# Cross-attention on one core: x exchanged a group earlier, first loads split, GpSimd's cutting of the weights put behind its norms

## The chip, the core and the metric

The kernel runs on one core of a Trainium2 chip, as one launch. The metric is device time in microseconds (us). The engines are TensorE (PE in the profile, its weight loads PEld), VectorE (DVE), ScalarE (ACT), GpSimd (POOL) and SyncE (SP, which here only issues DMAs). They run side by side and wait for one another on semaphores.

## What is computed

Two decoder layers with the norm behind each residual. The change touches the second stage alone:

```python
x = layernorm(x + self_attn(x))          # stage A
# cross-attention, 32 query heads on 8 key heads of width 16, keys = values = ctx_512
qh = x.reshape(4, 512, 8, 4, 16);  kh = vh = ctx_512.reshape(4, 512, 8, 16)
w  = softmax(einsum('bkgsd,bktd->bkgst', qh, kh) / 4)
x  = layernorm(x + einsum('bkgst,bktd->bkgsd', w, vh))   # stage B, this change
x  = layernorm(x + ffn(x))               # stage F: weights cut to -1, 0, 1 by their mean size
```

Stage B has 4 batches of 512 tokens. Beside its own work it prepares the weights of stage F: their mean absolute size is summed, and each weight is compared with half of it.

## The kernel before

`stage_cross_attention` works in 32 groups: 4 batches (b) of 8 key heads (j), a group being the 4 query heads of one key head. `plan` is one list, written out by loops, that PE, ACT and DVE all follow.

- Start of a batch's queries: PE turns x (units `xt`, two halves), ACT rounds the turned half to `XTH`, DVE takes the rest to `XTL`. SP writes both to DRAM (`XP`, `unload_x`) and reads them back stacked into 48 rows of `QS` (`stack_queries`, six DMAs a group). This is the exchange of x. Keys go the same way, once per half batch: `CH`, `CL` to `CP`, then into `KS` (`stack_keys`, six DMAs).
- A group g has 8 `max` units of group g+1 or g+2 (PE product, DVE reduce L921), one `mt` unit (PE turns the maxima, DVE copies them to `mT` at L930, SP puts them as a row into `QS` by `shift_row`), 16 score products `S` (L1001), each followed by an exp on ACT (L870), four products with the values `P`, and a `turn` unit by which DVE divides and writes the output `Z`. The first `S` of a group waits for the row of its `mt` (`shifted`).
- `M` has two buffers and `T` three, so that PE, DVE and ACT hold one another in step.
- The norm of a batch: GpSimd adds x to `Z` (L830), DVE makes the moments (four `bn_stats` and 25 small steps, two taken behind each `max` unit by `next(pending)`), then GpSimd applies them (L833). The last batch is done by DVE alone at the end (L949 to L953).
- GpSimd also cuts the weights in 12 chunks (`cut_weights`: L817, L818, L822, then a DMA to `ffn_w`). The order on GpSimd is that of its program: chunks 0 and 1, sum and norm of batch 0, chunks 2 to 6, sum and norm of batch 1, chunks 7 to 11, sum and norm of batch 2. The stage ends when every engine has ended, and stage F begins behind a barrier.
- At the start SP loads the context in two DMAs, waits for ACT and DVE, writes `CP` and `XP`, waits for both, and then stacks keys and queries. PE waits at its top for four memsets of GpSimd (`ones_set`).

Of the kernel before, what the change touches and what calls it, by code (L numbers as in the profile page):

```python
# [4 lines left out]
F32 = mybir.dt.float32  # L5
# [4 lines left out]
ALU = mybir.AluOpType  # L10
ACT = mybir.ActivationFunctionType
# [584 lines left out]
def stage_cross_attention(nc, X, C, A, FW):  # L596
# [21 lines left out]
    with ctx:  # L618
# [78 lines left out]
        drained = lambda kind, arg: at[kind, arg] + 3  # L697

        block = ctx.enter_context(nc.Block())

        @block.sync
        def _(sp):
            sp.dma_start(CT[:], A["ctxT"].rearrange("b e s -> e b s")).then_inc(ctx_in, 16)
            sp.dma_start(CTOK[:].rearrange("p (b i) e -> p b i e", b=NB),
                         A["ctx_512"].rearrange("b (i p) e -> p b i e", p=P)).then_inc(tok_in, 16)

            def unload_x(b):
                sp.wait_ge(hi_done, 2 * b + 2)
                sp.dma_start(XP[b % 2][0], XTH[:].bitcast(F32)).then_inc(x_out, 16)
                sp.wait_ge(m_free, drained("xt", (b, 1)))  # L710
                sp.dma_start(XP[b % 2][1], XTL[:].bitcast(F32)).then_inc(x_out, 16)
                sp.wait_ge(x_out, 32 * (b + 1))

# [8 lines left out]

            def stack_keys(b, lo, hi):
                for r in range(2):
                    for n, part in enumerate((0, 1, 0)):
                        rows = slice(LOW * r + HD * n, LOW * r + HD * (n + 1))
                        src = CP[part][HD * lo:HD * hi, b, :].rearrange("(j d) s -> d j s", d=HD)
                        sp.dma_start(KS[rows, lo:hi].bitcast(F32), src).then_inc(keys[lo], 16)

            def shift_row(g):  # L730
# [5 lines left out]

            sp.wait_ge(ctx_hi, 1)
            sp.dma_start(CP[0], CH[:].bitcast(F32)).then_inc(ctx_out, 16)
            sp.wait_ge(ctx_lo, 1)
            sp.dma_start(CP[1], CL[:].bitcast(F32)).then_inc(ctx_out, 16)  # L740
            unload_x(0)
            sp.wait_ge(ctx_out, 32)
            sp.wait_ge(ones_set, 4)
            stack_keys(0, 0, 4)
            stack_queries(0)
            stack_queries(1)
            stack_keys(0, 4, 8)
            stack_queries(2)
            shift_row(0)
            for g in range(GROUPS):  # L750
                b, j = g // KV, g % KV
                if g >= 1:
                    sp.wait_ge(t_full, STEPS_S * g)
                if j == 5 and b + 1 < NB:
                    unload_x(b + 1)
                    stack_keys(b + 1, 0, 4)
                if g + 3 < GROUPS:
                    stack_queries(g + 3)
                if j == 0 and b >= 1:
                    stack_keys(b, 4, 8)  # L760
                if g + 1 < GROUPS:
                    shift_row(g + 1)

        @block.gpsimd
        def _(pool):
# [25 lines left out]

            def sum_weights():
                fetch(0)
                fetch(1)
# [43 lines left out]
        @block.scalar  # L838
        def _(act):
            act.wait_ge(ctx_in, 16)  # L840
            ac.activation(CH[:], CT[:], ACT.Copy).then_inc(ctx_hi, 1)
            act.sem_inc(t_free, 3)
            act.sem_inc(o_free, 1)
            act.wait_ge(tok_in, 16)
            act.wait_ge(ones_set, 4)

            def make_values(b):
                if b >= 2:
# [5 lines left out]
            make_values(0)  # L854
            for x in plan:
                if x[0] == "M" and x[1] == "xt":
                    b, half = x[2]
                    act.wait_ge(m_full, at["xt", x[2]] + 1)
                    if b >= 1:
                        act.wait_ge(x_out, 32 * b)  # L860
                    ac.activation(XTH[:, 2 * half:2 * half + 2, :].rearrange("p k s -> p (k s)"),
                                  M[at["xt", x[2]] % 2][:], ACT.Identity).then_inc(hi_done, 1)
                elif x[0] == "S":
                    g, s = x[1:]
                    if g % KV == 6 and s == 0 and g // KV + 1 < NB:
                        make_values(g // KV + 1)
# [3 lines left out]
                    ac.activation(PT[:, s // 4, head(s), :], T[(STEPS_S * g + s) % 3][:], ACT.Exp, scale=SCALE).then_inc(t_free, 1)  # L870
                    if g < 6 and s % 4 == 2:
                        piece = 4 * g + s // 4
                        c, half = piece // 2, piece % 2
# [11 lines left out]
        @block.vector  # L885
        def _(dve):
            dve.wait_ge(ctx_hi, 1)
            ve.tensor_tensor(CL[:].rearrange("p b s -> p (b s)"), CT[:].rearrange("p b s -> p (b s)"),
                             CH[:].bitcast(F32).rearrange("p b s -> p (b s)"), ALU.subtract).then_inc(ctx_lo, 1)
            dve.sem_inc(m_free, 2)  # L890
            step = Steps(dve, norm, 0, GROUPS + 1 + NT)
# [14 lines left out]
            for n, x in enumerate(m_units):  # L906
# [3 lines left out]
                if kind == "xt":  # L910
                    b, half = arg
                    dve.wait_ge(hi_done, 2 * b + half + 1)
                    if b >= 1:
                        dve.wait_ge(x_out, 32 * b)
                    ks = slice(2 * half, 2 * half + 2)
# [3 lines left out]
                elif kind == "max":  # L919
# [4 lines left out]
                    if delay < 0:  # L924
                        next(pending, None)
                        next(pending, None)
                elif kind == "mt":
                    if arg >= 1:
                        dve.wait_ge(shifted, 32 * arg)
                    ve.tensor_copy(mT[:, :], m[0:4 * NT, 0:P]).then_inc(m_free, 1)  # L930
                elif kind == "turn":
                    o = m[:, 0:S].rearrange("p (i h d) -> p i h d", i=NT, h=4)
# [11 lines left out]
                    if j == KV - 1:  # L944
                        delay, pending = 5, layernorm_moments(b)

# [11 lines left out]
        def _(t):  # L958
            t.wait_ge(ones_set, 4)
            for x in plan:  # L960
                if x[0] == "M":
# [1513 lines left out]
```

## Time and profile before

| | |
|---|---|
| median of 3 runs | 2573.51 us (2572.28 to 2574.54) |
| the profiled execution | 2594.45 us |
| its span | 2592.7 us |
| PE, DVE, ACT, POOL busy | 2025.5, 1739.4, 1247.0, 771.5 us |

The busy times are over the whole kernel; stage B is the stretch from 486.96 us (its first instructions) to 1049.66 us (DVE's last norm). A row of the timeline gives the start, the duration of the merged instructions, the engine, the line, what it writes and reads, how many there are, and in brackets how long the engine was idle before and what ended that. The names of stage B's tiles begin with `x_`. Times between two rows of the same kind show the pace of the groups.

### The profile page before, as it was taken

The numbers are of one execution on the slowest core, as the hardware profiler recorded it, in microseconds if no ns is written. First come the engines' busy times: TensorE is split into PE (matmuls) and PEld (weight loads), VectorE is DVE, ScalarE is ACT, GpSimd is POOL, SyncE is SP. The second block draws the span as 40 slices with busy tenths as digits, with TensorE's granted clock in tenths as the row PEclk, the third lists the DMA queues.
The fourth block names the chain that finished last, engine by engine and source line by source line (L and its number), as shares of the span: only waits on it lengthen the run. The fifth ranks groups of instructions, "written<-read, shape, count | busy, mean of one in ns | idle before, by whom it ended". The sixth has DMA issues, their size and how long they took to land. (4 is left out here: it accounts for less than half of the span.)

```text
span 2592.7 us, 33108 instructions
## 1 busy us (share of the span) xinstructions
PE 2025.5 (78%) x12220; PEld 1362.0 (53%) x12252; DVE 1739.4 (67%) x2695; ACT 1247.0 (48%) x2228; POOL 771.5 (30%) x872
## 2 busy tenths in 40 slices
PE   5999999377778787688887499999940479889990
PEld 4777787222222222355554378787830357667760
DVE  3546565376767675789997445556659855379986
ACT  2233232167555556367777423223229541178971
POOL 1111213201594950121110121122315204055525
PEclk8899999678888989899997689999975789889995
DMA  5332322456343420400000332223210030099966
GB/s 154 82 74 50 74 50 50 142 143 175 86 142 88 143 59 7 185 1 1 1 1 1 98 73 65 56 53 74 50 65 1 0 117 1 4 408 423 414 276 194
DMA packets 84591, 264.62 MB, mean 102 GB/s; under 512 B 17504, under 2 KB 19040, under 8 KB 73424
## 3 DMA queue, kind: packets, MB, share of 16 engines
q0 software_dynamic: 29632, 151.50, 17.5%
q1 hardware_dynamic: 53776, 110.75, 15.1%
q8 instruction: 99, 1.62, 0.3%
q14 instruction: 60, 0.49, 0.1%
q10 hardware_dynamic: 1024, 0.26, 0.0%
HBM read 169.87 MB, written 41.72 MB: 82 GB/s over the span
## 5 line engine op out<-in xcount | busy, mean ns | idle before, releaser
L921 DVE TENSOR_REDUCE x_negm<-x_M 128x2 f32<-128x1024 f32 x256 | 309.4, 1224 | 112.8 <-PE x_M L981 112.2
L870 ACT ACTIVATE x_PT<-x_T 128x512 f32<-128x512 f32 x512 | 279.9, 598 | 201.5 <-PE x_T L1001 196.3
L327 ACT ACTIVATE L_attn_PT<-L_attn_T 128x512 f32<-128x512 f32 x320 | 175.5, 595 | 359.0 <-PE L_attn_T L559 359.0
L409 DVE TENSOR_REDUCE L_attn_negm<-L_attn_M 128x2 f32<-128x1024 f32 (+1 forms) x192 | 192.1, 1041 | 57.2 <-PE L_attn_M L540 57.1
L234 POOL DMA_DIRECT2D L_attn_QKS<-L_attn_HL x64 | 34.8, 544 | 599.0 <-ACT L_attn_HL L312 565.1
L1001 PE MATMUL x_T<-x_QS,x_KS 49*128 49x512 f32 x512 | 141.1, 548 | 64.5 <-ACT x_PT L870 44.9
L557 PE MATMUL L_attn_T<-L_attn_QKS 97*128 97x256 f32 (+3 forms) x512 | 166.2, 386 | 8.4 <-DMA L_attn_QKS<-L_attn_mT 6.1
L1001 PEld LDWEIGHTS x_T<-x_QS,x_KS 49*128 49x128 f32 x512 | 52.1, 200 | 214.4 <-ACT x_PT L870 131.2
L1010 PE MATMUL x_O<-x_PT,x_V 128*32 128x512 f32 x1024 | 155.6, 684 | 8.3 <-issue 8.3
L538 PE MATMUL L_attn_M<-L_attn_QKS 96*128 96x384 f32 (+2 forms) x384 | 139.7, 434 | 28.1 <-DVE L_attn_XTL L383 11.5
L981 PE MATMUL x_M<-x_KS,x_QS 48*128 48x512 f32 x512 | 119.1, 463 | 42.1 <-DMA x_QS<-x_xl 23.4
L2200 DVE TENSOR_TENSOR slots_WL<-slots_RAW,slots_WH 128x1024 fp32r<-128x1024 f32 x94 | 114.1, 1216 | 14.3 <-ACT slots_WH L2160 14.3
L559 PE MATMUL L_attn_T<-mask_kq,identr 128*128 128x128 f32 x512 | 121.3, 249 | 0.0
L2138 POOL DMA_INDIRECT slots_XG<-moe_x_rows,moe_slot_token x47 | 75.9, 1615 | 142.1 <-DVE slots_WL L2219 83.0
L557 PEld LDWEIGHTS L_attn_T<-L_attn_QKS 97*128 97x128 f32 x512 | 105.6, 206 | 15.2 <-DMA L_attn_QKS<-L_attn_mT 7.4
L437 DVE RECIPROCAL L_attn_AQ<-L_attn_DEN 128x512 f32<-128x512 f32 (+1 forms) x34 | 107.5, 3160 | 8.6 <-PE L_attn_O L583 8.6
L466 PE MATMUL L_attn_M<-L_attn_XTH,L_attn_WH 128*128 128x512 f32 x256 | 108.0, 422 | 6.1 <-DVE L_attn_WL L367 6.1
L1591 PE MATMUL graph_P<-graph_L,ident 128*128 128x512 f32 x32 | 18.3, 657 | 120.2 <-DVE graph_L L1664 120.2
L559 PEld LDWEIGHTS L_attn_T<-mask_kq,identr 128*128 128x128 f32 x512 | 106.9, 209 | 0.2
L2160 ACT ACTIVATE slots_WH<-slots_RAW 128x1024 fp32r<-128x1024 f32 x94 | 94.4, 1059 | 23.3 <-DMA slots_RAW<-in_experts,moe_weight_row 23.3
L538 PEld LDWEIGHTS L_attn_M<-L_attn_QKS 96*128 96x128 f32 x384 | 81.2, 211 | 45.3 <-DVE L_attn_XTL L383 14.5
L466 PE MATMUL L_attn_M<-L_attn_XTH,L_attn_WL 128*128 128x512 f32 x256 | 104.8, 409 | 0.0
(394 smaller groups left out, 5568.0 us busy)
## 6 DMA issues: line engine op xcount, KB each, us to landing
L_attn_QKS<-L_attn_HL SPq DMA_DIRECT2D x192, 128.0 KB, 4.7
L_attn_QKS<-L_attn_HL POOLq DMA_DIRECT2D x192, 128.0 KB, 3.9
moe_y_rows<-slots_YS SPq DMA_DIRECT2D x47, 256.0 KB
x_WRAW<-in_w_gateT POOLq DMA_DIRECT2D x8, 1024.0 KB, 7.5
x_QS<-x_xh SPq DMA_DIRECT2D x128, 64.0 KB, 2.4
x_WRAW<-in_w_upT POOLq DMA_DIRECT2D x8, 1024.0 KB, 5.2
x_WRAW<-in_w_downT POOLq DMA_DIRECT2D x8, 1024.0 KB, 6.3
ffn_w<-x_WTER POOLq DMA_DIRECT2D x12, 512.0 KB, 3.7
```

What stands on the lines that cost most here:

```text
L327: ac.activation(PT[:, s, bank], T[:, bank], ACT.Exp, scale=SCALE).then_inc(t_free, 1)
L409: last = ve.tensor_reduce(negm[:, g % 2, h0:h0 + nh, i], src, AX.X, ALU.max, negate=True)
L466: inst = pe.matmul(out, lhs(a, k), rhs(a, k), start=(k == 0 and a == 0), stop=(k == KC - 1 and a == 2))
L538: pe.matmul(m[:, c:c + w], QKS[0:R, r, 0, h, P * i:P * (i + 1)], QKS[0:R, r, 1, h, 0:w], start=True, stop=False)
L557: pe.matmul(T[:, c:c + w], QKS[0:R + 1, r, 1, h, P * j:P * (j + 1)], QKS[0:R + 1, r, 0, h, P * j:S], start=True, stop=False)
L559: last = pe.matmul(T[:, c:c + P], C["identr"][:], C["mask_kq"][:], start=False, stop=True)
L870: ac.activation(PT[:, s // 4, head(s), :], T[(STEPS_S * g + s) % 3][:], ACT.Exp, scale=SCALE).then_inc(t_free, 1)
L921: ve.tensor_reduce(negm[:, g % 2, u // 4:4:2, u % 4], m[:].rearrange("p (r k) -> p r k", r=2), AX.X, ALU.max, negate=True).then_inc(m_free, 1)
L981: last = pe.matmul(m[:, BANK * r:BANK * (r + 1)], QS[rows, g % 4, u // 4, P * (u % 4):P * (u % 4 + 1)], KS[rows, g % KV, :], start=True, s ...
L1001: pe.matmul(T[(STEPS_S * g + s) % 3][:], KS[rows, g % KV, P * j:P * (j + 1)], QS[rows, g % 4, head(s) % 2, :], start=True, stop=True).then ...
L1010: last = pe.matmul(O[VW * h:VW * (h + 1), :], V[:, (g // KV) % 2, j, g % KV, :], PT[:, j, h, :], start=(j == 0), stop=(j == NT - 1))
L2200: ve.tensor_tensor(WL[t % 2][:, cols], RAW[t % RING][:, cols], WH[t % 2][:, cols].bitcast(F32), ALU.subtract).then_inc(up_lo, 1)
```

## The change

It does these things, all in stage B:

- The `xt` units stand in group 3 of a batch and no longer in group 4; `unload_x` follows in SP's round j = 4 behind the queries of that round, and the wait for its landing and the keys stand in round j = 5.
- The first loads are cut: only batch 0 of the context comes first, the other three batches and the tokens later. ACT's queue, not SP's, writes batch 0's keys out and stacks them. SP writes x of batch 0 in two halves and stacks the queries of groups 0 and 1 after the first. DVE makes `CL` of batches 1 to 3 in groups 0 to 2, one behind each `mt`. PE waits for the memsets only at its first `max`.
- GpSimd's first two weight loads wait for the first row of maxima; ACT's 24 size pieces stand two places later.
- On GpSimd the chunks stand behind the norm of a batch: sum and norm 0, chunks 0 and 1, sum and norm 1, chunks 2 to 4, sum and norm 2, chunks 5 to 11.
- The moments begin one `max` unit earlier; the first four units take one step each, the later ones two.

```diff
-                if in_batch == 4 and s in (11, 13) and b + 1 < NB:
+                if in_batch == 3 and s in (11, 13) and b + 1 < NB:
...
+            def unload_first_x(half):
+                ks = slice(2 * half, 2 * half + 2)
+                sp.wait_ge(hi_done, half + 1)
+                sp.dma_start(XP[0][0][:, ks, :], XTH[:, ks, :].bitcast(F32)).then_inc(x_out, 16)
+                sp.wait_ge(m_free, drained("xt", (0, half)))
+                sp.dma_start(XP[0][1][:, ks, :], XTL[:, ks, :].bitcast(F32)).then_inc(x_out, 16)
...
+            unload_first_x(0)
+            sp.wait_ge(x_out, 32)
             stack_queries(0)
             stack_queries(1)
-            stack_keys(0, 4, 8)
+            ctx_tokens = A["ctx_512"].rearrange("b (i p) e -> p b i e", p=P)
+            sp.dma_start(CTOK[:, 0:NT, :], ctx_tokens[:, 0]).then_inc(tok_in, 16)
+            sp.dma_start(CT[:, 1:NB, :], ctxT[:, 1:NB, :]).then_inc(rest_in, 16)
+            shift_row(0)
             stack_queries(2)
-            shift_row(0)
+            sp.dma_start(CTOK[:, NT:, :].rearrange("p (b i) e -> p b i e", b=NB - 1), ctx_tokens[:, 1:]).then_inc(more_in, 16)
+            unload_first_x(1)
...
                 if j == 5 and b + 1 < NB:
-                    unload_x(b + 1)
-                    stack_keys(b + 1, 0, 4)
+                    sp.wait_ge(x_out, 32 * (b + 3))
...
+                    stack_keys(sp, b + 1, 0, 4)
                 if g + 3 < GROUPS:
                     stack_queries(g + 3)
+                if j == 4 and b + 1 < NB:
+                    unload_x(b + 1)
...
             def sum_weights():
+                pool.wait_ge(shifted, 32)
...
-            for b in range(NB - 1):
-                cut_weights((range(0, 2), range(2, 7), range(7, 12))[b])
+            for b, chunks in enumerate((range(0, 2), range(2, 5), range(5, 12))):
                 pool.wait_ge(m_free, drained("turn", KV * b + KV - 1))
...
+                cut_weights(chunks)
...
+                    if x[2] == (0, 1):
+                        act.wait_ge(ctx_hi, 1)
+                        act.dma_start(CP[0][:, 0:1, :], CH[:, 0:1, :].bitcast(F32)).then_inc(ctx_out, 16)
+                        act.wait_ge(ctx_lo, 1)
+                        act.dma_start(CP[1][:, 0:1, :], CL[:, 0:1, :].bitcast(F32)).then_inc(ctx_out, 16)
+                        act.wait_ge(ones_set, 4)
+                        act.wait_ge(ctx_out, 32)
+                        stack_keys(act, 0, 0, 4)
+                        stack_keys(act, 0, 4, 8)
...
                     if delay < 0:
                         next(pending, None)
+                    if delay < -NT:
                         next(pending, None)
...
+                    if 1 <= arg < NB:
+                        dve.wait_ge(ctx_hi, 2)
+                        split_context(slice(arg, arg + 1))
...
-                        delay, pending = 5, layernorm_moments(b)
+                        delay, pending = 4, layernorm_moments(b)
```

On GpSimd, before, the end of its part of stage B: the last chunk, the sum and norm of batch 2, and the branch that leaves the stage.

```order
L817 TENSOR_SCALAR x_WTER<-x_WRAW,x_cut 128x2048
L818 TENSOR_SCALAR x_WTER<-x_WRAW,x_cut 128x2048
L822 TENSOR_TENSOR x_WTER<-x_WTER 128x2048
L824 DMA ffn_w<-x_WTER 128x2048
L830 TENSOR_TENSOR x_Z<-x_Z,X 128x2048
L833 TENSOR_SCALAR X<-x_Z,x_x_ln_mean,x_x_ln_rstd 128x512 x4
L618 UNCONDITIONAL_BRANCH
```

The same place after, from the sum of batch 2 on (its first chunk is shown; six more like it follow).

```order
L845 TENSOR_TENSOR x_Z<-x_Z,X 128x2048
L848 TENSOR_SCALAR X<-x_Z,x_x_ln_mean,x_x_ln_rstd 128x512 x4
L833 TENSOR_SCALAR x_WTER<-x_WRAW,x_cut 128x2048
L834 TENSOR_SCALAR x_WTER<-x_WRAW,x_cut 128x2048
L793 DMA x_WRAW<-in_w_upT 128x2048
L838 TENSOR_TENSOR x_WTER<-x_WTER 128x2048
L840 DMA ffn_w<-x_WTER 128x2048
```

The norm of batch 2 was GpSimd's last work in the stage; now seven chunks, 5 to 11, stand behind it.

On SP, before, the start of the stage up to the second queries.

```order
L703 DMA x_CT<-in_ctxT 128x4x512
L704 DMA x_CTOK<-in_ctx 128x16x128
L738 DMA x_ch<-x_CH 128x2048
L740 DMA x_cl<-x_CL 128x2048
L709 DMA x_xh<-x_XTH 128x2048
L711 DMA x_xl<-x_XTL 128x2048
L728 DMA x_KS<-x_ch 16x4x512
L728 DMA x_KS<-x_cl 16x4x512
L728 DMA x_KS<-x_ch 16x4x512 x2
L728 DMA x_KS<-x_cl 16x4x512
L728 DMA x_KS<-x_ch 16x4x512
L721 DMA x_QS<-x_xh 16x2x512 x2
```

The same place after.

```order
L712 DMA x_CT<-in_ctxT 128x512
L723 DMA x_xh<-x_XTH 128x1024
L725 DMA x_xl<-x_XTL 128x1024
L734 DMA x_QS<-x_xh 16x2x512 x2
L734 DMA x_QS<-x_xl 16x2x512
L734 DMA x_QS<-x_xh 16x2x512 x2
L734 DMA x_QS<-x_xl 16x2x512
```

The keys and their 1 MB writes have left SP's queue for ACT's, and half of x is written before the first queries.

On DVE, before, the moments of batch 0 from their first step on.

```order
L94 BN_STATS x_x_ln_stats<-x_Z 128x6 x2
L921 TENSOR_REDUCE x_negm<-x_M 128x2
L94 BN_STATS x_x_ln_stats<-x_Z 128x6 x2
L921 TENSOR_REDUCE x_negm<-x_M 128x2
L64 TENSOR_TENSOR x_x_ln_mean<-x_x_ln_stats 128x4
L65 TENSOR_TENSOR x_x_ln_tmp<-x_x_ln_stats 128x4
```

The same place after.

```order
L94 BN_STATS x_x_ln_stats<-x_Z 128x6
L955 TENSOR_REDUCE x_negm<-x_M 128x2
L94 BN_STATS x_x_ln_stats<-x_Z 128x6
L955 TENSOR_REDUCE x_negm<-x_M 128x2
L94 BN_STATS x_x_ln_stats<-x_Z 128x6
L955 TENSOR_REDUCE x_negm<-x_M 128x2
L94 BN_STATS x_x_ln_stats<-x_Z 128x6
```

Four units carry one `bn_stats` each, where two carried two.

## Rows read from the trace of the kernel before

**Rows 1.** Waits from 495 to 1040 us: total, times, longest.

```profile
PE x_T L1001 <- DMA x_QS<-x_mT: 19.5, 5, 5.9
...
DVE x_x_ln_stats L94 <- POOL x_Z L830: 7.3, 2, 4.9
```

**Rows 2.** Timeline of the stage's start: start, duration, engine, line, operation.

```profile
486.96 1.81 POOL L766 MEMSET x_V<- 128x2048 f32 x1 [16.26 <-POOLq L48]
...
492.58 1.91 ACT L841 ACTIVATE x_CH<-x_CT 128x2048 fp32r<-128x2048 f32 x1 [6.72 <-DMA x_CT<-in_ctxT]
...
496.22 3.67 PE L971 MATMUL x_M<-ident,X 128*128 128x128 f32 x16 [21.30 <-POOL x_V L772]
...
498.23 1.02 ACT L861 ACTIVATE x_XTH<-x_M 128x1024 fp32r<-128x1024 f32 x1 [1.21 <-PE x_M L971]
499.36 1.23 DVE L916 TENSOR_TENSOR x_XTL<-x_M,x_XTH 128x1024 fp32r<-128x1024 f32 x1 [2.54 <-ACT x_XTH L861]
...
512.27 0.32 SPq L728 DMA_DIRECT2D x_KS<-x_ch  x1
...
523.26 1.22 PE L981 MATMUL x_M<-x_KS,x_QS 48*128 48x512 f32 x4 [23.36 <-DMA x_QS<-x_xl]
```

**Rows 3.** DMA queues, 512 to 532 us: packets, MB, share of 16 engines.

```profile
q1 hardware_dynamic: 1722, 2.63, 99.5%
```

**Rows 4.** The page's DMA issues: KB each, median us to landing.

```profile
ffn_w<-x_WTER POOLq DMA_DIRECT2D x12, 512.0 KB, 3.7
```

**Rows 5.** Timeline of DVE, the copies of the maxima around the three exchanges.

```profile
620.45 0.27 DVE L930 CAST x_mT<-x_M 16x128 fp32r<-16x128 f32 x1
...
643.71 0.27 DVE L930 CAST x_mT<-x_M 16x128 fp32r<-16x128 f32 x1
...
752.87 0.27 DVE L930 CAST x_mT<-x_M 16x128 fp32r<-16x128 f32 x1
...
775.73 0.27 DVE L930 CAST x_mT<-x_M 16x128 fp32r<-16x128 f32 x1
...
882.00 0.27 DVE L930 CAST x_mT<-x_M 16x128 fp32r<-16x128 f32 x1
...
902.65 0.27 DVE L930 CAST x_mT<-x_M 16x128 fp32r<-16x128 f32 x1
...
915.77 0.27 DVE L930 CAST x_mT<-x_M 16x128 fp32r<-16x128 f32 x1
```

**Rows 6.** The same copies around the moments of batches 0 and 1.

```profile
671.08 0.27 DVE L930 CAST x_mT<-x_M 16x128 fp32r<-16x128 f32 x1
...
721.72 0.27 DVE L930 CAST x_mT<-x_M 16x128 fp32r<-16x128 f32 x1
...
801.94 0.27 DVE L930 CAST x_mT<-x_M 16x128 fp32r<-16x128 f32 x1
...
850.92 0.27 DVE L930 CAST x_mT<-x_M 16x128 fp32r<-16x128 f32 x1
```

**Rows 7.** Timeline of GpSimd's chunks, sums and last norm, and DVE's end.

```profile
772.32 5.46 POOL L817 TENSOR_SCALAR x_WTER<-x_WRAW,x_cut 128x2048 bf16<-128x2048 f32 x1
...
806.05 4.56 POOL L830 TENSOR_TENSOR x_Z<-x_Z,X 128x2048 f32<-128x2048 f32 x1
...
851.19 5.43 POOL L817 TENSOR_SCALAR x_WTER<-x_WRAW,x_cut 128x2048 bf16<-128x2048 f32 x1
...
929.09 4.09 POOL L822 TENSOR_TENSOR x_WTER<-x_WTER 128x2048 bf16<-128x2048 bf16 x1
...
970.13 8.24 POOL L833 TENSOR_SCALAR X<-x_Z,x_x_ln_mean,x_x_ln_rstd 128x512 f32<-128x512 f32 x4 [31.44 <-DVE x_x_ln_rstd L77]
...
1047.37 2.29 DVE L953 TENSOR_SCALAR X<-x_Z,x_x_ln_mean,x_x_ln_rstd 128x512 f32<-128x512 f32 x4
```

**Rows 8.** Two stretches: PE, PEld, DVE, ACT, POOL busy; PEclk, DMA share, GB/s.

```profile
820.00:835.00 15.00, 14.22 (x58) 4.04 (x51) 9.50 (x21) 6.91 (x13) 0.00 (x0) 0.50 0.10 27
840.00:855.00 15.00, 12.15 (x83) 4.09 (x81) 12.57 (x19) 10.85 (x21) 12.05 (x5) 1.00 0.10 28
```

More of the change, by code:

```diff
@@ L697, in stage_cross_attention, with stack_keys @@
         drained = lambda kind, arg: at[kind, arg] + 3
+        def stack_keys(queue, b, lo, hi):
+            for r in range(2):
+                for n, part in enumerate((0, 1, 0)):
+                    rows = slice(LOW * r + HD * n, LOW * r + HD * (n + 1))
+                    src = CP[part][HD * lo:HD * hi, b, :].rearrange("(j d) s -> d j s", d=HD)
+                    queue.dma_start(KS[rows, lo:hi].bitcast(F32), src).then_inc(keys[lo], 16)
         block = ctx.enter_context(nc.Block())
@@ L721, in stack_queries @@
                         sp.dma_start(QS[rows, g % 4].bitcast(F32), src).then_inc(stacked[g % 4], 16)
[L723 to L728, printed above, removed]
             def shift_row(g):
@@ L753, in _ @@
                     sp.wait_ge(t_full, STEPS_S * g)
+                if g == 1:
+                    sp.wait_ge(x_out, 64)
+                if g == 3:
+                    sp.wait_ge(ctx_hi, 2)
+                    sp.dma_start(CP[0][:, 1:NB, :], CH[:, 1:NB, :].bitcast(F32)).then_inc(ctx_out, 16)
+                    sp.wait_ge(ctx_lo, NB)
+                    sp.dma_start(CP[1][:, 1:NB, :], CL[:, 1:NB, :].bitcast(F32)).then_inc(ctx_out, 16)
                 if j == 5 and b + 1 < NB:
-                    unload_x(b + 1)
-                    stack_keys(b + 1, 0, 4)
+                    sp.wait_ge(x_out, 32 * (b + 3))
+                    if b == 0:
+                        sp.wait_ge(ctx_out, 64)
+                    stack_keys(sp, b + 1, 0, 4)
                 if g + 3 < GROUPS:
                     stack_queries(g + 3)
+                if j == 4 and b + 1 < NB:
+                    unload_x(b + 1)
                 if j == 0 and b >= 1:
-                    stack_keys(b, 4, 8)
+                    stack_keys(sp, b, 4, 8)
                 if g + 1 < GROUPS:
@@ L839, in _ @@
         def _(act):
-            act.wait_ge(ctx_in, 16)
-            ac.activation(CH[:], CT[:], ACT.Copy).then_inc(ctx_hi, 1)
             act.sem_inc(t_free, 3)
             act.sem_inc(o_free, 1)
-            act.wait_ge(tok_in, 16)
-            act.wait_ge(ones_set, 4)
+            act.wait_ge(ctx_in, 16)
+            ac.activation(CH[:, 0, :], CT[:, 0, :], ACT.Copy).then_inc(ctx_hi, 1)
+            sizes = [(n // 4, 4 * (n % 4) + 2) for n in range(2, 26)]
             def make_values(b):
+                act.wait_ge(more_in if b else tok_in, 16)
                 if b >= 2:
@@ L859, in _ @@
                     if b >= 1:
-                        act.wait_ge(x_out, 32 * b)
+                        act.wait_ge(x_out, 32 * (b + 1))
                     ac.activation(XTH[:, 2 * half:2 * half + 2, :].rearrange("p k s -> p (k s)"),
                                   M[at["xt", x[2]] % 2][:], ACT.Identity).then_inc(hi_done, 1)
+                    if x[2] == (0, 1):
[7 more added lines that the diff above has]
+                        stack_keys(act, 0, 4, 8)
                 elif x[0] == "S":
                     g, s = x[1:]
+                    if g == 0 and s == 4:
+                        make_values(0)
+                    if g == 0 and s == 0:
+                        act.wait_ge(rest_in, 16)
+                        ac.activation(CH[:, 1:NB, :], CT[:, 1:NB, :], ACT.Copy).then_inc(ctx_hi, 1)
                     if g % KV == 6 and s == 0 and g // KV + 1 < NB:
@@ L870, in _ @@
                     ac.activation(PT[:, s // 4, head(s), :], T[(STEPS_S * g + s) % 3][:], ACT.Exp, scale=SCALE).then_inc(t_free, 1)
-                    if g < 6 and s % 4 == 2:
-                        piece = 4 * g + s // 4
+                    if (g, s) in sizes:
+                        piece = sizes.index((g, s))
                         c, half = piece // 2, piece % 2
@@ L886, in _, with split_context @@
         def _(dve):
+            dve.sem_inc(m_free, 2)
+            def split_context(bs):
+                ve.tensor_tensor(CL[:, bs, :].rearrange("p b s -> p (b s)"), CT[:, bs, :].rearrange("p b s -> p (b s)"),
+                                 CH[:, bs, :].bitcast(F32).rearrange("p b s -> p (b s)"), ALU.subtract).then_inc(ctx_lo, 1)
             dve.wait_ge(ctx_hi, 1)
[L888 to L890 removed]
+            split_context(slice(0, 1))
             step = Steps(dve, norm, 0, GROUPS + 1 + NT)
@@ L974, in _ @@
                         g, u = arg
+                        if arg == (0, 0):
+                            t.wait_ge(ones_set, 4)
                         if u == 0:
```

21 lines of the change are left out of this document (5 added, 16 removed).

## The prediction, as it was written before the run

> **What bounds the kernel now.** I read the page first, then the waits of PE and DVE inside stage B, then the timeline, which gives the price of each wait. By the page PE is busy 78% of the whole kernel, but that share says nothing of one stage. Stage B runs from its first memset at 486.96 us [rows 2] to the end of DVE's last norm at 1047.37 + 2.29 = 1049.66 us [rows 7], 562.7 us. In between, groups without anything extra follow each other every 13.12 us (902.65 to 915.77) [rows 5]; PE, DVE and ACT hold one another there, and the change leaves that pace alone. What it goes for are three kinds of gap.
>
> The start: PE's first transpose waits 21.30 us for GpSimd's last memset, and its first product with keys waits another 23.36 us for queries, until 523.26 [rows 2]. The exchanges: of the five waits of PE for the row of maxima, 19.5 us in all, three are of 5 to 6 us and stand where SP first waited for x to land [rows 1]; the groups there take 23.26, 22.86 and 20.65 us [rows 5]. The norms: DVE waits 7.3 us in two places for GpSimd's sum [rows 1].
>
> GpSimd has slack at the end: its last norm is at 970.13 and takes 8.24 us, and the stage ends 79.53 us after that norm's start, by DVE [rows 7]. The change moves GpSimd's work into this slack.
>
> **The start.** PE's transposes no longer wait. Half of them take 3.67 / 2 = 1.84 us, so the first half is turned at 488.8. The full context came 492.58 - 486.96 = 5.6 us after the stage's start for 1 MB [rows 2], 512 KB take 3.7 [rows 4]; a quarter MB I put at 3.0 (2.8 by the same line, 3.7 at most), so 490.0. ACT rounds it (a quarter of 1.91 us, say 0.6 with its latency) and then the half of x, 1.02: 491.6. DVE's rest of it, 1.23: 492.9 [rows 2]. Writing 512 KB takes 3.7: 496.6, and GpSimd's memsets end at 496.2. I take 497 for the first stacking DMAs, where 512.27 stands now: 15.3 us.
>
> From the first stacking DMA to the first product there are 11.0 us now (523.26 - 512.27) [rows 2]: 768 KB of keys and 384 KB of queries in one queue, at 2.63 MB in 20 us = 132 GB/s, with the engines' time 99.5% taken [rows 3]. Now keys come from ACT's queue beside two groups of queries from SP's. If each queue kept 132 GB/s, the keys would be there after 768 KB / 132 = 5.8 and a landing, 7.5 us; if both share 132, after 1.54 MB, 11.6 + 1.1 = 12.7 us. I take 9, nearer the lower end, because a DMA here writes only 16 partitions and two queues write different ones. The start gains 15.3 + 2.0 = 17.3 us (13.6 to 18.8).
>
> The Trainium skill speaks against my 9: in "DMA: Bandwidth & Descriptors", section "Issuing engines are not separate DMA queues", it says that DMAs of several issuing engines run on the same 16 DMA engines and interleave, so that only issue time is saved. By that rule alone the 12.7 holds and the start gains 13.6; this trace agrees in that the one queue fills the engines' time to 99.5% [rows 3]. That is a rival below.
>
> Beside it: the rest of the context, the tokens, the second half of x and two 1 MB weight loads come in the first 16 us of the scores, in front of the row of group 1. I charge 0.5 us (0 to 3). DVE's three pieces of `CL` are a quarter of the size of the work that was done at the start; each is about half of an `xt` rest of 1.23 us, 0.6, three make 1.8 if nothing hides them and 0 if the gaps between reduces do; I take 1.0. ACT's pieces are only moved by two places, GpSimd's first loads by a wait that ends before they are needed: 0.
>
> **The exchanges.** Above 13.12 us the three groups have 10.1, 9.7 and 7.5 us, 27.4 together [rows 5]. Now SP writes x a whole group earlier and in round j = 5 finds it landed. It then issues twelve DMAs, 1.15 MB, 8.7 us at 132 GB/s, before the maxima are copied; the row follows behind them and may still be late by a little, 1 us each by my choice (0 to 2). The transposes cost what they did, one group earlier. They hold PE up too, so one stretch at the low clock (5.1 us, worked out below) may stay where PE's long wait is gone; I leave half of one in, 2.5. 27.4 - 3 - 2.5 = about 22 us (18 to 27).
>
> **The norms.** The sum on GpSimd now comes at once, so the 7.3 us of waiting go. They are not worth 7.3: from 671.08 to 721.72, with a wait of 4.9, it takes 50.64 us, and from 801.94 to 850.92, with none, 48.98 [rows 6]. Two thirds of a wait are made good by the buffers, so 1.9 us for both. Spreading: two units with two `bn_stats` become four with one, 0.5 us less each, and the moments end one unit (1.6 us) later, which counts for batch 2 only: +1.0 and -1.1. Together 1.8.
>
> In these stretches PE's clock falls to 1.2 GHz: from 820 to 835 it is granted 0.50 and PE issues 58 matmuls, from 840 to 855 it is granted 1.00 and issues 83 [rows 8]. So 17 us at the low level lose 17 x (1 - 58/83) = 5.1 us. It fell after the units with two `bn_stats` had held PE up. With one each PE is held less, and I expect one of the three falls to go: 5 us (0 to 15).
>
> **What is late next.** Behind the norm of batch 2 GpSimd now has seven chunks. Two take 806.05 - 772.32 = 33.7 us, five take 929.09 + 4.09 - 851.19 = 82.0 [rows 7]. Then 0.3 us and the landing of the last 512 KB, 3.7 [rows 4], for which GpSimd waits. From the start of that norm: 8.24 + 33.7 + 82.0 + 4.0 = 127.9 us, where DVE needs 79.53. The stage therefore ends 48.4 us later than DVE would end it, and stage F, behind the barrier, has nothing to cover it. All gains count only as far as they bring the norm of batch 2 forward, and all of the above do.
>
> **Sum.** 17.3 + 22 + 1.8 + 5 - 1.5 = 44.6 us earlier, 48.4 later: +3.8 us. The profiled execution goes from 2594.45 to 2598.3. It stands 0.8% over the median; the difference carries over as it is, 2573.51 + 3.8 = 2577.3, say 2577.5. By the bounds of the terms this case reaches from -3 to +10 us. A measurement can tell about 0.2%, 5.15 us, from no change, so this case is mostly "the same".
>
> **Rivals.**
> - The clock falls in all three norms as before. For it: DVE's work is the same 29 steps, and PE is held in any case. Against: the held units get shorter. Price +5.1: +8.8, 2582.3. It decides on the slower side once none of the three falls goes and the start and exchanges come as forecast; this is the case in which the tail of GpSimd, 48.4 us, beats the gains by more than a measurement's width.
> - The clock stays at 2.4 GHz in all three: 10 us more, -6.4, 2567. For it: the longest hold of PE in a norm, DVE's wait for the sum, is gone. Against: one norm had no such wait [rows 6] and its clock fell all the same, at 820 [rows 8].
> - Both queues share 132 GB/s at the start: first product at 509.7, 3.7 us less gained, +7.5, 2581. For it the 99.5% [rows 3], against it the 16 partitions.
> - GpSimd's tail is hidden, that is, the chunks are quicker when DVE rests, or fit: then the full 44.6 are gained, 2529. Against: the five chunks took the same time whatever DVE did [rows 7].
> - DVE's last norm is held up by GpSimd's chunks, which now run beside it: it has 18 instructions with two SBUF inputs in its last 12.5 us; even if each waited for the end of a 5.4 us instruction, they would be through about 5.5 us after the last chunk's compute, 1.5 us after GpSimd's own landing: +5.3, 2578.8. The Trainium skill has this rule in "SBUF — State Buffer", section "Who interferes with whom": such a DVE instruction and a GpSimd one that reads SBUF exclude each other. No row above shows it.
>
> **Chances.** The forecast 0.37, clock falls in all 0.25, in none 0.20, shared queues 0.10, tail hidden 0.05, DVE held 0.03. From 2565 to 2589 holds all but the hidden tail and the edges. Faster by over 0.2%: nearly all of the tail hidden, two thirds of the clock held, a little of the forecast, 0.22. Slower: four fifths of the clock falling, two thirds of the shared queues, a third of the forecast, 0.40. The rest, 0.38, is within 0.2%.
>
> **What would show it.** First product with keys 17.5 to 22.8 us after the stage's first instruction, where it is 36.3 now; no wait over 2 us of PE for the row of maxima; no wait of DVE for GpSimd's sum; GpSimd's seven chunks running back to back for about 116 us behind the norm of batch 2, while DVE has ended some 48 us before the stage does. The forecast is wrong if GpSimd is not the last engine of the stage, if a chunk takes other than 16 to 17 us, or if the norm of batch 2 starts elsewhere than 40 to 50 us earlier.

## The result, and the profile after

The changed kernel takes 2585.07 us (median of 20 runs, 2571.93 to 2610.5) where the kernel before takes 2574.97 in the same session (20 runs, 2570.57 to 2581.7): ratio 1.0042, 95% interval 1.0026 to 1.0057. It is slower by 10.1 us by the medians and 10.8 us by the ratio; 3.8 were forecast. The experiments ran in four later sessions, each on a chip of its own; in the first of them the ratio is the same, 1.0041 (1.0019 to 1.0062), at a level 18 us higher.

The two profiled executions (2594.45 and 2597.25 us) differ by only 2.8 us, and that misleads. From SP's first row in each stage: stage B has become 18.4 us longer (from 486.96 to 1050.85 before, 563.9; from 488.59 to 1070.88 after, 582.3), and the stages from the graph to the combining of experts 16.5 us shorter, without any change there. The waits of PE in those stages of the kernel before account for most of that; no row of this kind stands in those of the changed kernel:

```profile
PE share_UG L2051 <- issue: 10.7, 9, 2.1
```

PE waited there for nothing that the profile shows, and its clock fell with it (0.70 on the mean from 2190 to 2210 us, where the changed kernel has 1.00). A total of one execution therefore can't be used here; from now on stage B is read by itself, with times from its first instruction.

The start of stage B after the change, from the timeline of all engines (start, duration, engine, line, tile, count, idle before and its releaser):

```profile
488.59 0.35 SPq L712 DMA_DIRECT2D x_CT<-in_ctxT  x1
488.69 3.67 PE L1008 MATMUL x_M<-ident,X 128*128 128x128 f32 x16 [12.14 <-DVEq L917]
...
497.83 0.33 ACTq L705 DMA_DIRECT2D x_KS<-x_ch  x1
...
498.60 0.79 SPq L734 DMA_DIRECT2D x_QS<-x_xh  x2
...
510.29 1.22 PE L1020 MATMUL x_M<-x_KS,x_QS 48*128 48x512 f32 x4 [17.93 <-DMA x_QS<-x_xl]
```

The first stacking DMA of keys comes 9.2 us after the stage's start (10.0 forecast), the first product with keys 21.7 (19.0 forecast, 36.3 before [rows 2]). Between the two lie 12.5 us, where 9 were taken.

The wait of PE for the row of maxima (all of stage B: us in all, times, longest), against 19.5, 5 and 5.9 before [rows 1]:

```profile
PE x_T L1040 <- DMA x_QS<-x_mT: 2.6, 2, 1.8
```

What stands in its place is PE's clock. The stretches of 10 us around the turn of x for batch 1 (columns: length, then busy us and instructions of PE, weight loads, DVE, ACT, GpSimd, then granted clock, DMA share, GB/s):

```profile
686.00:696.00 10.00, 8.37 (x59) 2.56 (x58) 9.18 (x14) 7.16 (x14) 3.98 (x2) 1.00 0.16 42
696.00:706.00 10.00, 7.48 (x49) 3.73 (x53) 5.90 (x11) 5.42 (x9) 10.00 (x5) 0.96 0.01 2
706.00:716.00 10.00, 9.48 (x40) 2.40 (x32) 7.13 (x6) 5.49 (x11) 9.68 (x3) 0.50 0.83 309
716.00:726.00 10.00, 9.47 (x41) 3.28 (x37) 5.63 (x10) 4.34 (x8) 9.66 (x4) 0.50 0.27 104
```

686 to 696 is the norm of batch 0, where the kernel before fell to the low clock; now it keeps 2.4 GHz. Up to 703.62 PE waits 1.77 us for DVE to empty the buffer with the turned x, and from 706 it runs at 1.2 GHz with 40 matmuls in 10 us instead of 59. The group that contains the turn takes 21.10 us and the next one 17.86, where 13.12 is the pace [rows 5].

GpSimd at the end (timeline of POOL; its norm of batch 2, the first and the last of seven chunks, then stage F):

```profile
938.80 8.24 POOL L848 TENSOR_SCALAR X<-x_Z,x_x_ln_mean,x_x_ln_rstd 128x512 f32<-128x512 f32 x4 [33.80 <-DVE x_x_ln_rstd L77]
947.03 5.43 POOL L833 TENSOR_SCALAR x_WTER<-x_WRAW,x_cut 128x2048 bf16<-128x2048 f32 x1
...
1047.62 5.45 POOL L833 TENSOR_SCALAR x_WTER<-x_WRAW,x_cut 128x2048 bf16<-128x2048 f32 x1
1053.04 5.61 POOL L834 TENSOR_SCALAR x_WTER<-x_WRAW,x_cut 128x2048 bf16<-128x2048 f32 x1
1058.73 4.09 POOL L838 TENSOR_TENSOR x_WTER<-x_WTER 128x2048 bf16<-128x2048 bf16 x1
1063.12 0.69 POOL L840 DMA_DIRECT2D ffn_w<-x_WTER  x1 [0.30 <-POOL x_WTER L838]
1070.57 0.09 POOL L1162 MEMSET ffn_magic<- 128x1 f32 x1 [6.76 <-POOLq L48]
```

The seven chunks take 1062.82 - 947.03 = 115.8 us, as forecast. From the norm's start to stage F's first row on GpSimd it is 131.8 us (by SP's first row, which the table below goes by, 132.1). The norm starts 450.2 us after the stage's start, 33.0 earlier than before [rows 7]; in a second profile 442.9, 40.3 earlier.

DVE meanwhile, behind its last turn (the same 39 instructions took 13.5 us before, 1036.20 to 1049.66):

```profile
1005.19 3.88 DVE L987 TENSOR_TENSOR x_Z<-x_Z,X 128x2048 f32<-128x2048 f32 x1
...
1014.10 0.17 DVE L66 TENSOR_TENSOR x_x_ln_var<-x_x_ln_stats 128x4 f32<-128x4 f32 x1
1014.30 0.17 DVE L67 TENSOR_SCALAR x_x_ln_mean<-x_x_ln_mean 128x4 f32<-128x4 f32 x1
1014.50 3.99 DVE L68 TENSOR_TENSOR x_x_ln_tmp<-x_x_ln_tmp 128x4 f32<-128x4 f32 x1
1018.53 1.70 DVE L69 TENSOR_SCALAR x_x_ln_var<-x_x_ln_var 128x4 f32<-128x4 f32 x1
1020.26 3.65 DVE L70 SCALAR_TENSOR_TENSOR x_x_ln_var<-x_x_ln_tmp,x_x_ln_var 128x4 f32<-128x4 f32 x1
...
1047.34 16.35 DVE L991 TENSOR_SCALAR X<-x_Z,x_x_ln_mean,x_x_ln_rstd 128x512 f32<-128x512 f32 x4
```

An operation on 128x4 numbers, 0.17 us by itself, takes up to 4.75 us when it meets an instruction of GpSimd, and the four pieces of the norm take 16.35 us instead of 2.29. DVE needs 59.4 us from its last turn (1004.25) to 1063.69. It still ends before GpSimd's landing, so this costs nothing here.

### The profile page after: what moved, and what is told of

Same layout as the page of the kernel before. It is cut to its first block and busy times, and to the rows that moved or that the text cites. A ratio compares the mean times of both kernels' runs of the same rounds, so it can differ in the third digit from the quotient of the medians.

```text
span 2594.9 us, 33152 instructions
## 1 busy us (share of the span) xinstructions
PE 2029.2 (78%) x12252; PEld 1361.3 (52%) x12252; DVE 1784.2 (69%) x2698; ACT 1247.8 (48%) x2229; POOL 772.9 (30%) x872
## 3 DMA queue, kind: packets, MB, share of 16 engines
q1 hardware_dynamic: 54672, 108.65, 14.7%
```

## The experiments

All ratios are to the kernel before on the same chip; the texts of expectation speak in us of the first session, so ratios are compared. "Stage B" and "norm 2" (the start of GpSimd's norm of batch 2, from the stage's start) are of one profiled execution of each kernel; the changed kernel's are those of its second profile (its first has 582.3 and 450.2).

| start | exchange | GpSimd's chunks | ratio (95%) | stage B | norm 2 | DVE waits for sums |
|---|---|---|---|---|---|---|
| old | old | ahead of sums 2, 5, 5 (before) | 1 | 563.9 | 483.2 | 7.3 |
| new | old | ahead of sums | 1.0002 (0.9981-1.0023) | 564.0 | 483.2 | 20.6 |
| old | new | ahead of sums | 0.9988 (0.9968-1.0008) | 563.9 | 479.8 | 25.1 |
| new | new | ahead of sums | 1.0004 (0.9987-1.0021) | 557.6 | 477.9 | 33.9 |
| old | old | behind norms 2, 3, 7 | 1.0140 (1.0118-1.0162) | 597.3 | 465.6 | 0 |
| new | old | behind norms 2, 3, 7 | 1.0129 (1.0109-1.0148) | 581.5 | 448.5 | 0 |
| new | new | behind norms 2, 3, 7 (after) | 1.0041 (1.0019-1.0062) | 575.1 | 442.9 | 0 |
| old | old | behind norms 4, 4, 4 | 0.9939 (0.9912-0.9966) | 549.1 | 462.4 | 0 |
| old | new | behind norms 4, 4, 4 | 0.9870 (0.9837-0.9904) | 544.8 | 458.1 | 0 |
| new | old | behind norms 4, 4, 4 | 0.9904 (0.9871-0.9936) | 530.9 | 449.2 | 0 |
| new | new | behind norms 4, 4, 4 | 0.9864 (0.9834-0.9895) | 521.1 | 439.1 | 0 |

The moments go with the rows: they stand as before wherever the start is old and in the second row, and as in the change elsewhere.

**The changed kernel again.**

> The changed kernel once more, for a second profile. Theory 1 (GpSimd's tail ends the stage): whatever the gains ahead are in this execution, stage B ends 131.8 us after the start of GpSimd's norm of batch 2 (131.8 in the first profile, 938.80 to 1070.57); the time is 2585 us, within 10. Theory 2 (DVE, held up by GpSimd's chunks, ends the stage): that distance follows DVE's end and scatters by several us.

Measured: 2601.21 against 2593.39 us on this chip. From norm 2 to stage F's first row on GpSimd 131.9 us (131.8 in the first profile), though the norm came 7.3 us sooner. The distance is fixed: theory 1. The end of DVE's last norm keeps its distance too (124.9 us in the first profile, 125.0 in this one), so the scatter does not tell the two theories apart; that DVE is through 6.9 us before stage F in both does.

**Four chunks behind each norm.**

```
-            for b, chunks in enumerate((range(0, 2), range(2, 5), range(5, 12))):
+            for b, chunks in enumerate((range(0, 4), range(4, 8), range(8, 12))):
```

> GpSimd cuts four chunks behind each of its three norms, where the changed kernel has two, three and seven. Theory 1 (the seven chunks end the stage, and nothing behind covers them): GpSimd ends its four at 947 + 4 x 16.8 + 4 = 1018 us by the first profile's clock, DVE at 1004 + 12.5 + some 5 of waiting for GpSimd = about 1020; stage B ends 49 us earlier and the time is 2585 - 49 = 2536 us (2528 to 2545). Theory 2 (what the changed kernel loses, it loses ahead of the tail, by the low clock and the exchanges): the time stays above 2570.

Measured: ratio 0.9864 against 1.0041, 46 us less; stage B ends 82 us behind norm 2 and not 132. The long tail costs more than the whole loss of 10 us, and this version beats both kernels. Its end (timeline of POOL and DVE):

```profile
993.19 4.26 POOL L838 TENSOR_TENSOR x_WTER<-x_WTER 128x2048 bf16<-128x2048 bf16 x1
997.75 0.59 POOL L840 DMA_DIRECT2D ffn_w<-x_WTER  x1 [0.30 <-POOL x_WTER L838]
1005.80 0.09 POOL L1162 MEMSET ffn_magic<- 128x1 f32 x1 [7.45 <-POOLq L48]
```
```profile
990.80 2.74 DVE L987 TENSOR_TENSOR x_Z<-x_Z,X 128x2048 f32<-128x2048 f32 x1
...
1002.10 0.16 DVE L77 TENSOR_TENSOR x_x_ln_rstd<-x_x_ln_rstd,x_x_ln_tmp 128x4 f32<-128x4 f32 x1
1002.30 2.29 DVE L991 TENSOR_SCALAR X<-x_Z,x_x_ln_mean,x_x_ln_rstd 128x512 f32<-128x512 f32 x4
```

With GpSimd's compute over at 997.45 DVE's small steps take 0.16 us again and its norm 2.29. So it was GpSimd's running that stretched them.

**The chunks back ahead of the sums, the rest changed.**

```
-            for b, chunks in enumerate((range(0, 2), range(2, 5), range(5, 12))):
+            for b, chunks in enumerate((range(0, 2), range(2, 7), range(7, 12))):
+                cut_weights(chunks)
                 pool.wait_ge(m_free, drained("turn", KV * b + KV - 1))
...
-                cut_weights(chunks)
```

> The changed kernel with GpSimd's chunks where they stood before (two, five and five, each time ahead of its sum of x), the rest changed. Theory 1: GpSimd has no tail, DVE ends the stage in 12.5 us behind its last turn; DVE waits again for two late sums, 5 us in all at most; 2585 - 53 + 5 = 2537 us (2530 to 2548), level with four chunks behind each norm. Rival: the norms' gain in the profile (19.5 us where 6.8 were forecast) comes from GpSimd being idle between sum and norm; then it goes too, and this is 10 to 15 us slower than four chunks behind each norm.

Measured: 1.0004. Both expectations are missed by far; the late sums were put at 5 us and are 33.9. The waits of DVE in stage B:

```profile
DVE x_x_ln_stats L94 <- POOL x_Z L846: 33.9, 3, 18.4
```

New start and new exchange together bring nothing as long as the chunks stand ahead of the sums. That called for each part alone.

**The new start alone** (the changed kernel with exchange, moments and GpSimd's order as before):

> The kernel before with the new start alone (split first loads, keys from ACT's queue); the exchange, the moments and GpSimd's order as before. Theory 1 (GpSimd's chunks stand in front of its sums and take over as soon as anything ahead of them gets shorter, as in the 33.9 us of waits of the last run): the start's 14.5 us are gone by the first norm, DVE waits 15 to 30 us for GpSimd's sums instead of 7.3; faster than before by 0 to 5 us. Rival (the forecast's sum, each term by itself): faster by 14 to 17 us.

Measured: 1.0002. The first cast of the maxima (DVE's copy to `mT`) comes 14.2 us earlier (33.16 us after the stage's start for 47.32), norm 2 at 483.2 as before. DVE waits 20.6 us for the sums as theory 1 has it, 17.5 of them in the norm of batch 0. There GpSimd's timeline shows:

```profile
649.94 5.44 POOL L832 TENSOR_SCALAR x_WTER<-x_WRAW,x_cut 128x2048 bf16<-128x2048 f32 x1
...
682.93 0.57 POOL L839 DMA_DIRECT2D ffn_w<-x_WTER  x1 [0.30 <-POOL x_WTER L837]
683.53 4.52 POOL L845 TENSOR_TENSOR x_Z<-x_Z,X 128x2048 f32<-128x2048 f32 x1
```

The first chunk can begin only when the mean size of the weights is there. That is 163.5 us after the stage's start, 158.5 before the change. So the first sum comes 5.0 us later than before, though PE's groups up to there come 6 to 14 us earlier. The new start also has GpSimd's first loads wait and puts ACT's size pieces two places later; whether that is the reason was not tested. In the next norm DVE waits only 1.2 us, and there the rows are:

```profile
800.63 5.44 POOL L833 TENSOR_SCALAR x_WTER<-x_WRAW,x_cut 128x2048 bf16<-128x2048 f32 x1
806.36 0.83 POOL L792 DMA_DIRECT2D x_WRAW<-in_w_downT  x1 [0.30 <-POOL x_WTER L833]
807.21 4.08 POOL L837 TENSOR_TENSOR x_WTER<-x_WTER 128x2048 bf16<-128x2048 bf16 x1
811.59 0.55 POOL L839 DMA_DIRECT2D ffn_w<-x_WTER  x1 [0.30 <-POOL x_WTER L837]
812.15 4.57 POOL L845 TENSOR_TENSOR x_Z<-x_Z,X 128x2048 f32<-128x2048 f32 x1
842.26 8.26 POOL L848 TENSOR_SCALAR X<-x_Z,x_x_ln_mean,x_x_ln_rstd 128x512 f32<-128x512 f32 x4 [25.54 <-DVE x_x_ln_rstd L77]
```

The sum follows the fifth chunk without a gap here too. From a norm's start: 8.25 + five chunks 83 to 84 + sum and moments 30 to 37 make the next norm, 122.5 and 127.4 us in this run, 129.2 and 127.2 before the change. GpSimd's order was a loop of its own, about as long as eight groups of PE: with no chunk ahead of a sum (four behind each norm, below) the same two distances are 119.6 and 126.8 us with the old start and exchange, 118.1 and 118.3 with the new ones.

**The new exchange alone.**

```
-                if in_batch == 4 and s in (11, 13) and b + 1 < NB:
+                if in_batch == 3 and s in (11, 13) and b + 1 < NB:
...
                 if j == 5 and b + 1 < NB:
-                    unload_x(b + 1)
+                    sp.wait_ge(x_out, 32 * (b + 2))
                     stack_keys(b + 1, 0, 4)
                 if g + 3 < GROUPS:
                     stack_queries(g + 3)
+                if j == 4 and b + 1 < NB:
+                    unload_x(b + 1)
```

> The kernel before with the exchange of x one group earlier and nothing else. Theory 1: PE's waits for the row of maxima shrink from 19.5 to under 7 us, but DVE's waits for GpSimd's sums grow by as much as the exchanges gain (to 20 us or more); faster than before by 0 to 8 us. Rival (the forecast's term): faster by 22 us.

Measured: 0.9988. PE's waits for the row fall from 19.5 to 3.6 us, DVE's for sums rise to 25.1 (10.3, 8.6 and 6.2 in the three norms). Theory 1 holds for both parts.

**GpSimd's order alone**, with four, four and four and with two, three and seven chunks behind the norms:

```
             for b in range(NB - 1):
-                cut_weights((range(0, 2), range(2, 7), range(7, 12))[b])
...
+                cut_weights((range(0, 4), range(4, 8), range(8, 12))[b])
```

> The kernel before with GpSimd's order changed alone: four chunks behind each of its three norms, none ahead of a sum. Theory 1: DVE's waits for GpSimd go, but with the old start and exchanges they are only 7.3 us, and they are worth 2 to 11 us; GpSimd's four last chunks end behind the norm of batch 2 after 8 + 67.5 + 4 = 80 us, level with DVE: faster by 2 to 12 us. Rival (the order by itself is worth what the profiles show in the norms, 19.5 us): faster by 15 to 20 us.

Measured: 0.9939, 16 us faster, above theory 1's 2 to 12 and in the rival's span: norm 2 comes 20.8 us earlier, for waits of 7.3. With the wait a fall of the clock goes: the three groups around the norm of batch 0 take 41.1 us instead of 52.1. The fall in the norm of batch 1, where DVE had not waited at all, is gone as well (the two groups from 801.94 us on took 36.1 us, now 28.0); the fall in the norm of batch 2 stays. With two, three and seven chunks (next) the fall of batch 1 is back, so it does not hang on the wait. The stretches around it, of this kernel and then of the kernel before:

```profile
685.00:695.00 10.00, 8.37 (x62) 2.74 (x54) 9.45 (x21) 6.90 (x13) 0.00 (x0) 1.00 0.14 40
695.00:705.00 10.00, 8.35 (x54) 2.70 (x53) 8.90 (x19) 6.71 (x13) 2.82 (x2) 1.00 0.15 42
```
```profile
685.00:695.00 10.00, 7.59 (x27) 2.69 (x27) 7.88 (x20) 2.86 (x6) 0.00 (x0) 0.50 0.00 1
695.00:705.00 10.00, 9.00 (x40) 2.72 (x42) 6.99 (x16) 5.36 (x11) 0.00 (x0) 0.59 0.14 39
```

> The kernel before with GpSimd's order of the change alone (two, three and seven chunks behind its norms). Theory 1 (the tail is a fixed length behind the norm of batch 2, and the order by itself brings that norm 20.8 us forward, 483.2 to 462.4, as with four chunks behind each norm): stage B takes 462.4 + 132 = 594 us, 30.5 more than before; ratio to before 1.010 to 1.013. Rival (GpSimd's seven chunks are quicker, or the norm comes earlier, with fewer chunks between the norms): under 1.008.

Measured: 1.0140, stage B 597.3, 131.7 us behind norm 2, which came at 465.6. The tail is as long as expected, the norm 3 us later, so the ratio stands just above theory 1's 1.013.

**The moments as before, the rest changed** (first step one unit later, two a unit).

> The changed kernel with the moments as before (first taken up one unit later, two a unit). Theory 1 (spreading is worth at most 1 or 2 us and shifts the low clock by chance): within 4 us of the changed kernel, 2581 to 2589 where that has 2585. Rival (the spreading kept PE's clock up in the first norm, 17 us at the low level, 5 us each): slower than the changed kernel by 5 to 15 us.

Measured: 1.0033 (1.0010 to 1.0056), norm 2 at 452.6. Not to be told from the changed kernel; the rival's 5 to 15 us are not there. In its profile PE keeps 1.00 through the norm of batch 0 (657 to 699 us), so the spreading is not what keeps the clock up there.

**The exchange undone, with the long tail and with the short one.**

> The changed kernel with the exchange of x in the place that it had before (x turned in the fifth group of a batch, unloaded and waited for by SP in the sixth). Theory 1 (by the profiles the earlier exchange was worth 5.5 us of the 22 forecast, since PE's clock falls in it all the same): 2585 + 5.5 = 2590 us (2586 to 2597), PE waits again some 10 to 20 us for the row of maxima. Rival (the forecast's own term): 2585 + 22 = 2607 us.

Measured: 1.0129, which is 0.9% or 23 us over the changed kernel and the rival's number; PE waits 17.3 us for the row again. But its profiled execution was the fastest of seven, and its stage B is 6.4 us over the changed kernel's second profile and 0.8 us under its first.

> Four chunks behind each norm, the new start, the exchange in its old place. Theory 1 (by the difference of the two timed kernels with GpSimd's long tail, 22.6 us): ratio to before 0.986 + 0.009 = 0.995. Rival (by the profiles, 6 to 13 us): 0.989 to 0.991.

Measured: 0.9904, 10 us over the kernel with all parts. The three timed pairs that differ in the exchange alone and have GpSimd's new order give 23, 10 and 18 us (1.0129 - 1.0041, 0.9904 - 0.9864, 0.9939 - 0.9870), each within some 8 to 12 us. Taken together they show that it is worth something there; how much, between 10 and 23, stays open.

**The old start and the old moments, the rest changed.**

> Four chunks behind each norm, the exchange one group earlier, the start and the moments as before. With GpSimd's order changed nothing stands behind its queue any more, so here the start shows by itself. Theory 1 (the start's 14.5 us at the first cast, less 4 to 5 for the low clock behind it): 9 to 11 us slower than the kernel with all three parts (which stands at 0.986 of before), ratio to before about 0.990. Rival (the start's gain is swallowed elsewhere even so): ratio 0.985 to 0.988.

Measured: 0.9870, inside the rival's span; theory 1's 0.990 lies within the interval too (0.9837 to 0.9904), so there is no verdict. The profiles have norm 2 at 458.1 against 439.1, 19 us, of which the times show 2. In the two other pairs that differ in start and moments and have GpSimd's new order the times show 9 us (0.9939 - 0.9904) and 3 us (1.0140 - 1.0129), where the profiles have norm 2 13.2 and 17.1 us sooner. Each pair is within some 8 to 12 us. So what the new start is worth in the whole kernel stays open: 2 to 9 us by the times, 13 to 19 by the profiles.

**Keys from SP's queue** instead of ACT's, four chunks behind each norm:

```
+            stack_keys(sp, 0, 0, 4)
             stack_queries(0)
             stack_queries(1)
+            stack_keys(sp, 0, 4, 8)
...
-                        stack_keys(act, 0, 0, 4)
-                        stack_keys(act, 0, 4, 8)
```

> Four chunks behind each norm and all of the change, but batch 0's keys stacked from SP's queue between its queries, as before, instead of from ACT's. Theory 1 (both queues share the 16 engines: from the first stacking DMA to the first product it took 12.5 us with two queues, 11.0 before with one): the first product comes 20 to 23 us after the stage's start as it does now (21.7), the time within 2 us of the kernel with keys from ACT's queue. Rival (a second queue brings what the forecast took from it): the first product comes 3 to 5 us later.

Measured: the first product 21.1 us after the stage's start (508.70 - 487.59), 21.7 with two queues; ratio 0.9829 (0.9796 to 0.9862), where its twin has 0.9864 (0.9834 to 0.9895); the intervals overlap. The second queue brings nothing that shows. One thing differs beside the queue: the second half of the keys now stands behind the first two groups' queries.

## Why the prediction was right, and where not

**Start: 17.3 forecast, 14.6 measured at the first cast, 9.3 to 10.2 by the fourth.** The first stacking DMA was right (9.2 us, 10.0 said). The step that failed is "I take 9" from there to the first product: it took 12.5, as the rival with shared queues had it (12.7), and one queue does as well (11.1, from 497.62 to 508.70). The Trainium skill's rule in "DMA: Bandwidth & Descriptors", section "Issuing engines are not separate DMA queues", is what the run with keys from SP's queue shows: 21.1 us with one queue, 21.7 with two. The next 4 to 5 us go to PE's clock, on which the forecast had no term here. In the first profile the clock came up at about 551 us, 27 us behind the first scores (9 us before, the last row below), and the third group took 19.32 us instead of 13.81 (17.87 in the second profile). The three rows of the changed kernel, then one of the kernel before:

```profile
526.00:536.00 10.00, 9.19 (x33) 2.93 (x37) 7.28 (x8) 6.71 (x14) 0.00 (x0) 0.50 0.99 323
536.00:546.00 10.00, 9.48 (x40) 2.40 (x32) 5.46 (x5) 6.78 (x13) 0.54 (x1) 0.50 0.75 250
546.00:556.00 10.00, 8.94 (x45) 3.13 (x41) 6.38 (x11) 7.05 (x14) 0.54 (x1) 0.72 0.39 128
```
```profile
546.00:556.00 10.00, 8.06 (x53) 2.42 (x49) 7.54 (x8) 9.34 (x18) 0.54 (x1) 0.99 0.60 195
```

PE is busy 9.48 of 10 us at 0.50 from 536 to 546, so here it is the clock and not a wait that costs. Why it came up so much later is open. In the whole kernel the timed pairs show only 2 to 9 us for the new start and the moments together.

**Exchanges: 22 forecast, 4 to 10 measured** by norm 2 in the profiles with a short tail (462.4 to 458.1; 449.2 to 439.1), 10 to 23 us by the timed pairs. PE's wait went as said (2.6 us are left). By the profiles the term was mis-sized in "I leave half of one in, 2.5" for the clock: in the changed kernel's first profile batch 1's turn alone brings 28 us at 1.2 GHz (705 to 733), and the two groups in it stand 8.0 and 4.7 us over the pace (6.1 and 0.0 in the second profile, where it is about 7 us). The timed pairs reach up to 23, so the 22 are not refuted.

**Norms and clock: 1.8 + 5 forecast, 20.8 and 17.6 measured** by norm 2 with the order alone (four, four, four and two, three, seven). The mis-sized step is "so 1.9 us for both": the waits of 7.3 us were read as what GpSimd cost. They said only by how much it was behind PE at that moment; and the clock came on top, as the rows at 685 to 705 show for the norm of batch 0. The row that would have told was there: the sum starts where the chunks end (772.32 + 33.7 = 806.05) [rows 7], so GpSimd had no slack between two norms. That one of three falls of the clock goes came true: 686 to 696 is at 1.00, the other two norms still fall. The reason given for it, one `bn_stats` a unit instead of two, did not hold: that fall is gone with GpSimd's order alone, and it stays away with the moments as before. Here the forecast was right by luck.

**The sum of the three: 44.6 forecast; 33.0 and 40.3 in the two profiles of the changed kernel, 44.1 with a short tail.** It came out near because all parts went in together, and in part by luck: by the profiles the exchanges were put 12 to 18 us too high and the norms with the clock 11 to 14 us too low. The terms stood as if each could be had alone; two of them are worth nothing that shows alone (1.0002, 0.9988), because GpSimd's chunks took their gain back as a longer wait of DVE (20.6 and 25.1 us). By the forecast's own signs the norm of batch 2 had to start 40 to 50 us earlier; 40.3 is just inside, the first profile's 33.0 is not.

**Tail: 48.4 forecast, 51 measured** (131.8 - 80.7). The chunks were right to 0.1 us. Short was the end: from the last compute to stage F 7.7 us, where 4.0 were put, taken from the median landing of 3.7 us, with no 1.2 us for the barrier, which DVE's end had too. The sign "DVE has ended some 48 us before the stage does" failed: DVE ended 6.9 us before it, for the reason under "DVE held up".

**Together:** gains of 40.3, a tail of 51.5 (by SP's rows): +11.2 us in the second profile (575.1 against 563.9), near the +10.1 to 10.8 of the timed runs. Both errors go to the slower side, 4.3 and 3.1 us on top of +3.8. The first profile has gains of 33.0 and +18.4 us; the fit of the second is that of one execution.

**DVE held up (0.03):** the mechanism is there, much larger than "18 instructions" suggests, and it does not decide: DVE ends 0.9 us after GpSimd's last compute (1063.69 and 1062.82) and 6.9 us before stage F. The Trainium skill, "SBUF — State Buffer", section "Who interferes with whom", says that a DVE instruction with two SBUF inputs and a GpSimd one that reads SBUF exclude each other, and that the fast forms of `tensor_scalar` take the shared ports too. The trace agrees on both as far as times can show it: where small steps were held, those with two inputs took 1.85 to 4.75 us, `tensor_scalar` 1.30 to 1.70, neither over 0.2 alone; the forecast had counted the first kind only.

## What to carry to other kernels

Before crediting a gain, look at what stands in front of each handshake on the engine that has to answer. An engine whose work between two answers runs back to back has no slack, however short the waits for it are, and a small wait is then no price but, as here, the sign of two chains of nearly equal length. When work is moved off such a chain, count what it comes to behind the last answer: here four chunks held DVE's end up by 0 to 2.6 us (from its last turn to stage F 14.7 to 17.2 us in five kernels, 14.7 before), and three more cost 46 us.

## What the runs showed of the hardware

- While GpSimd ran elementwise instructions back to back, DVE's last 39 instructions took 59.4 us instead of 13.5; GpSimd's own kept their 5.4 and 4.1 us, within 0.2.
- A two-input DVE instruction did not wait for the end of GpSimd's `tensor_scalar` of 5.46 us (1014.73 to 1020.19): it was through at 1014.50 + 3.99 = 1018.49, some 3.8 us into it. DVE's own `tensor_scalar` behind it was through at 1018.53 + 1.70 = 1020.23, with its end. The same 22 us later: from 3.7 us into GpSimd's instruction (1037.12 to 1042.55) two-input steps take their 0.16 us again, while the `tensor_scalar` is through at 1041.28 + 1.30 = 1042.58.

```profile
1037.21 3.64 DVE L77 TENSOR_TENSOR x_x_ln_rstd<-x_x_ln_rstd,x_x_ln_tmp 128x4 f32<-128x4 f32 x1
1040.88 0.16 DVE L74 TENSOR_TENSOR x_x_ln_tmp<-x_x_ln_rstd 128x4 f32<-128x4 f32 x1
1041.08 0.16 DVE L75 TENSOR_TENSOR x_x_ln_tmp<-x_x_ln_tmp,x_x_ln_var 128x4 f32<-128x4 f32 x1
1041.28 1.30 DVE L76 TENSOR_SCALAR x_x_ln_tmp<-x_x_ln_tmp 128x4 f32<-128x4 f32 x1
```

- A wait of PE of 1.8 us at the turn of x (batch 1) was followed by 28 us at 1.2 GHz in the first profile of the changed kernel and by about 7 us (703 to 710) in the second; the group behind that turn took 17.86 and 13.13 us. What decides between the two is open. The changed kernel's runs scatter over 39 us, those of the kernel before over 11 in the same session. That the old GpSimd order hid such falls is not shown: on another chip the kernel before scatters over 25 us in 35 runs, and with four chunks behind each norm over 27 in 12.
